# One output tile of the next quarter ahead of each loop over the rests of the counts, and a wait for attention's constants moved behind attention's first projection

## What is computed

```python
xn = layernorm(x)
# graph part: 20,000 edges, a self edge for every node
h   = xn @ W.T + b
out = segment_sum(deg**-0.5[row] * deg**-0.5[col] * h[col], row)
# attention part: 16 heads of 64, random features (exp of a projection)
q, k, v = xn @ Wq.T + bq, xn @ Wk.T + bk, xn @ Wv.T + bv
attn = phi(q) @ (phi(k).T @ v) / (phi(q) @ sum(phi(k)))
x = x + out + attn @ Wo.T + bo
# eight experts, the best two of each node are mixed
x = x + mixture_of_experts(layernorm(x))
```

## Time and profile before

| | |
|---|---|
| time, median of 3 runs | 1614.45 us (1612.59 to 1615.34) |
| the profiled execution, its own time | 1616.33 us |
| its span, first to last instruction | 1614.8 us |
| granted TensorE clock, mean | 0.949 |
| PE matmul busy | 1411.8 us, 87% of the span |
| DVE, ACT, POOL busy | 47%, 29%, 24% |
| graph stage, from the first matmul of line 1523 to the last | 312.9 to 449.7 us |
| share of PE in the chain that ended last | 76% |

### The profile page before, as it was taken

How to read it: one execution, slowest core, us unless ns; L and a number is a source line. 1 busy time by engine, 2 the same in 40 slices (tenths; PEclk the granted TensorE clock), 3 DMA queues, 4 the chain that set the end, 5 groups by cost and what they waited for, 6 DMA issues and landing times.

```text
span 1614.8 us, 26325 instructions
## 1 busy us (share of the span) xinstructions
PE 1411.8 (87%) x8396; PEld 1245.2 (77%) x8460; DVE 758.5 (47%) x1492; ACT 465.8 (29%) x777; POOL 383.8 (24%) x380
## 2 busy tenths in 40 slices
PE   5788878967879999999999999997999499999980
PEld 2566666967879999999999999996888488888860
DVE  7754443414334545444444545345454425444536
ACT  7412222401013333333232424243222113223310
POOL 7422343233221010101010101002224211222233
PEclk9999999988889999999999999999999599999995
DMA  4100111334222020202020202003144326665657
GB/s 150 54 32 23 53 59 56 97 115 123 84 71 85 20 90 14 91 13 91 13 91 13 91 13 78 0 1 120 57 144 139 141 74 237 239 238 215 213 199 279
DMA packets 64532, 158.06 MB, mean 98 GB/s; under 512 B 7978, under 2 KB 28922, under 8 KB 64032
## 3 DMA queue, kind: packets, MB, share of 16 engines
q1 hardware_dynamic: 55200, 127.20, 22.4%
q0 software_dynamic: 9280, 30.17, 6.0%
HBM read 119.98 MB, written 55.71 MB: 109 GB/s over the span
## 4 chain that ended last, share of the span: by engine, by line
PE 76%; DMA 7%; DVE 6%; issue 5%; ACT 2%; POOL 2%; DVEq 1%; SPq 1%; POOLq 0%; ACTq 0%
PE PB L1562 7%; PE PB L1564 7%; PE PB L1563 7%; PE PB L1738 5%; PE PB L1739 5%; PE PB L1741 5%; PE PB L1598 4%; PE PB L1621 4%; PE PB L1466 4%; DMA y_scratch<-xrow 3%; PE PB L1507 2%; PE PB L1544 2%; PE PB L1508 2%; PE PB L1509 2%; PE PB L1545 2%
## 5 line engine op out<-in xcount | busy, mean ns | idle before, releaser
L1562 PE MATMUL PB<-xh,hw 128*128 128x416 f32 (+1 forms) x576 | 206.0, 358 | 7.0 <-POOL orfl L758 7.0
L1564 PE MATMUL PB<-xh,hw 128*128 128x416 f32 (+1 forms) x576 | 204.1, 354 | 0.0
L1563 PE MATMUL PB<-xl,hw 128*128 128x416 f32 (+1 forms) x576 | 203.8, 354 | 0.0
L1738 PE MATMUL PB<-mwh,mth 128*128 128x512 f32 x368 | 149.4, 406 | 1.3 <-issue 1.3
L1466 PE MATMUL PB<-ohs,ohd 128*128 x471 | 107.4, 352 | 46.5 <-DVE ohs L1116 31.6
L1739 PE MATMUL PB<-mwl,mth 128*128 128x512 f32 x368 | 144.7, 393 | 0.0
L703 POOL CAST hw<-hraw 128x1024 fp32r<-128x1024 f32 x24 | 25.1, 1047 | 466.6 <-PE PB L1564 465.8
L1466 PEld LDWEIGHTS PB<-ohs,ohd 128*128 x534 | 52.3, 99 | 100.3 <-issue 82.3
L1562 PEld LDWEIGHTS PB<-xh,hw 128*128 128x128 f32 x576 | 109.4, 190 | 8.4 <-POOL orfl L758 7.2
L1741 PE MATMUL PB<-mwh,mtl 128*128 128x512 f32 x368 | 114.4, 392 | 0.0
L1563 PEld LDWEIGHTS PB<-xl,hw 128*128 128x128 f32 x576 | 109.5, 190 | 1.3
(11 more groups left out here) (260 smaller groups left out, 3135.3 us busy)
## 6 DMA issues: line engine op xcount, KB each, us to landing
mraw<-expert_w SPq DMA_DIRECT2D x64, 512.0 KB, 7.4
slot_y<-x SPq DMA_DIRECT2D x7, 2560.0 KB, 12.2
slot_y<-ybuf SPq DMA_DIRECT2D x46, 256.0 KB, 3.3
count_rests<-ATf POOLq DMA_DIRECT2D x9, 640.0 KB, 3.3
xrow<-x SPq DMA_DIRECT2D x40, 128.0 KB, 2.5
y_scratch<-xrow SPq DMA_DIRECT2D x40, 128.0 KB, 2.4
yrow<-y_scratch SPq DMA_DIRECT2D x20, 256.0 KB, 2.9
x2n_half<-xhat SPq DMA_DIRECT2D x20, 256.0 KB, 2.5
```

The costliest lines, as they stand in the source:

```text
L1562: mm(bank(i, n), hw[:, wi, 0, k, :], xh[:, k, c0:c0 + n], start=(k == 0), stop=False)
L1563: mm(bank(i, n), hw[:, wi, 0, k, :], xl[:, k, c0:c0 + n], start=False, stop=False)
L1564: ins = mm(bank(i, n), hw[:, wi, 1, k, :], xh[:, k, c0:c0 + n], start=False, stop=(k == KT - 1))
L1738: mm(y[c], mth[:, k, :], mwh[par][:, k, c * CW:(c + 1) * CW], start=(k == 0), stop=False)
```

## The change

On PE, DVE and POOL the loop over quarter q's rests now stands behind the first tile (t = 0) of quarter q + 1 and before its second; the last quarter's stays at the end. On POOL it was behind the second tile. PE's wait for `a_cst` stands behind `project(0, 0)`; ACT's and DVE's waits stay. The diff, without the lines that only move:

```diff
@@ POOL
             for u in range(TILES):
                 q = u // TT
+                if u % TT == 1 and u > TT:
+                    add_rests(q - 1)
                 pool.wait_ge(g_x[u % 4], 16 * (u // 4 + 1))
                 g.tensor_tensor(xrow[:, u % 4, :], xrow[:, u % 4, :], bob[:, q * QW:(q + 1) * QW], ALU.add).then_inc(xb_ready, 1)
                 if u in (TT, TT + 8):
                     split_head(0, (u - TT) // 8)
-                if u % TT == 1 and u > TT:
-                    add_rests(q - 1)
             add_rests(NQ - 1)
@@ DVE
             for u in range(TILES):
                 q, t = u // TT, u % TT
+                if t == 1 and q:
+                    take_rests(q - 1)
                 dve.wait_ge(g_done, u + 1)
                 dve.wait_ge(xb_ready, u + 1)
...
-                if t == TT - 1:
-                    with dve.Fori(0, rest_dve) as n:
...
+            take_rests(NQ - 1)
@@ PE
             for u in range(TILES):
                 q, t = u // TT, u % TT
+                if t == 1 and q:
+                    multiply_rests(q - 1)
...
                 ins.then_inc(g_done, 1)
-                if t == TT - 1:
-
-                    with pe.Fori(0, rest_pe) as n:
...
+            multiply_rests(NQ - 1)
@@ PE, attention
-
-            pe.wait_ge(a_cst, 7)
...
             project(0, 0)
+            pe.wait_ge(a_cst, 7)
             pairs(pe, pair)
```

More of the change, by code:

```diff
@@ L1152, in _, with take_rests @@
                     low_scaled(q, b)
+            def take_rests(q):
+                with dve.Fori(0, rest_dve) as n:
+                    b, at = rest_tile(n)
+                    k = rest_dve * q + n
+                    dve.wait_ge(rest_done, k + 1)
+                    dve.wait_ge(rest_over, k + START)
+                    v.tensor_scalar(resty[:, :], bank(3, QW), dis[:, ds(at, 1)], None, ALU.mult).then_inc(rest_taken, 1)
             for u in range(TILES):
                 q, t = u // TT, u % TT
+                if t == 1 and q:
+                    take_rests(q - 1)
                 dve.wait_ge(g_done, u + 1)
@@ L1512, in _, with multiply_rests @@
             rest_pe = rest_tiles(pe)
+            def multiply_rests(q):
+                with pe.Fori(0, rest_pe) as n:
+                    b, _ = rest_tile(n)
+                    k = rest_pe * q + n
+                    pe.wait_ge(rest_ready, 16 * (k + 1))
+                    pe.wait_ge(rest_taken, k + START)
+                    mm(bank(3, QW), restb[:, :], hh[:, q % 2, ds(b, 1), :].rearrange("p a n -> p (a n)"),
+                       start=True, stop=True).then_inc(rest_done, 1)
             for u in range(TILES):
                 q, t = u // TT, u % TT
+                if t == 1 and q:
+                    multiply_rests(q - 1)
                 at = slice(t * P, (t + 1) * P)
```

## The result

| | before | changed |
|---|---|---|
| time, median | 1613.52 us (4 runs) | **1597.35 us** (4 runs, 1596.04 to 1597.88) |
| ratio, 95% interval | | **0.9902** (0.9881 to 0.9922) |
| same comparison, beside e4, e5, e7 | 1614.24 us (11 runs) | 1603.15 us (6 runs), 0.9922 (0.9908 to 0.9936) |
| same comparison, beside e9, e10, e11 | 1615.85 us (9 runs) | 1599.73 us (5 runs), 0.9902 (0.9886 to 0.9918) |
| span of the profiled execution | 1614.8 us | 1596.3 us |

I had predicted 1602.6 us, with 1598.5 to 1609.0 as the range. The change is faster, as forecast, but by 16 us in the result's own comparison, and its time lies 1.2 us outside the range. Of the 5.3 us between forecast and time, 0.9 is the kernel before, whose median is 1613.52 us here and was 1614.45 when I predicted. Repeated, the change gave 11 and 16 us.

What follows compares the result with a forecast made beforehand. SP's ring was taken to pace the graph stage, with PE's wait for the constants ahead of attention. Borders -4.9 and constants -6.95 made -11.9 us; against 1614.45 that gave 1602.6 us, range 1598.5 to 1609.0.

Steps and rivals of the forecast that it cites:

- border 0/1: Between graph-stage quarters 0 and 1: rest loaded 0.6 us earlier, store of tile 11 0.1 us later; +1.7 with a slower DMA.
- border 1/2: Between graph-stage quarters 1 and 2: store of tile 21 1.3 us earlier, held by the load of hrf; ends -1.8 and +1.1.
- border 2/3: Between graph-stage quarters 2 and 3: rest loaded at 417.63 instead of 420.44, so the store of tile 31 3.7 us earlier.
- if that delay goes too, it is -5.1: Behind tile 31's store: the next load came 3.86 us later instead of 2.46; without that delay, -5.1 instead of -3.7 us.
- its cover: At attention's start: PE's first third, 7.72 us, would end 0.8 us behind the constants and so just hide them.
- the adding DMA: POOL's DMA in the chain of the rest at each border: issue to next addition put at 4.4, 6.04 and 3.44 us.
- Rival B: Adding DMA not held up by hrf, 3.44 us at each border: -0.9, -2.2 and -3.7, in all 1600.7 us; chance 0.12.
- SP's ring sets the pace: Graph stage: SP's stores and loads need 2.8 us a tile, PE 2.4, so most of PE's 34.9 us wait costs nothing.
- the constants' term: Attention's start: PE no longer waits for the constants ahead of its first projection, which starts 6.95 us earlier.
- rival D: Borders: a lost tile of lead lets the ring run dry, 6.4 us each; slower, 1626.7 us; chance 0.04.
- My far bounds: The fast ends of two terms: -6.8 us for the three borders, -7.2 us for the wait for the constants.
- rival C: Attention's start: DVE meets POOL's 2.37 us instruction, PE waits and 2.4 us go back, 1605.0 us; chance 0.06.

Runs made afterwards that it cites:

- e4: The changed kernel with the two loads of hrf issued from ACT's queue instead of SP's; 1604.99 us, ratio 0.9940 to the kernel before.
- e5: The changed kernel with POOL no longer waiting for the adding DMA's landing; ACT waits and signals instead; 1601.34 us, ratio 0.9919 to the kernel before.
- e7: The changed kernel with the diffs of e4 and e5 together; 1600.79 us, ratio 0.9908 to the kernel before.
- e9: The changed kernel with the last rest's matmul behind the first third of attention's first projection on PE; 1599.10 us, ratio 0.9905 to the kernel before.
- e10: The changed kernel with the diffs of e9 and e5 together; 1594.50 us, ratio 0.9868 to the kernel before.
- e11: The changed kernel with 16 matmuls without use on PE in its wait ahead of the last rest; 1599.20 us, ratio 0.9897 to the kernel before.
- e1: The kernel before with only PE's wait for the constants moved, the loops over rests left in place; 1608.74 us, ratio 0.9952.
- e3: The changed kernel with POOL's loop over rests again behind its addition of t = 1; 1602.29 us, ratio 0.9917 to the kernel before.
- e6: e2 with 50 matmuls without use on PE ahead of the wait for the constants; 1608.27 us, ratio 0.9952 to the kernel before.
- e2: The changed kernel with PE's wait for the constants put back, so only the loops moved; 1608.28 us, ratio 0.9956 to the kernel before.
- e8: The changed kernel again, unchanged, run beside e4, e5 and e7; ratio 0.9922 to the kernel before.
- e12: The changed kernel once more, unchanged, run beside e9, e10 and e11; ratio 0.9902 to the kernel before.

## Why the prediction was wrong, and what of it was right

The table sets my terms beside the profiles. The old order of the graph stage has two (the kernel before, and the one with only the constants moved, e1), the change has three. A border is from the store of tile 10 q - 1 to that of 10 q + 1; "quarters" are the rest of the first three.

| stretch, us | old order | change | difference of means | my term |
|---|---|---|---|---|
| border 0/1 | 10.95, 11.75 | 12.64, 12.25, 12.11 | +1.0 | +0.1 |
| border 1/2 | 11.77, 12.85 | 12.04, 12.16, 12.15 | -0.2 | -1.3 |
| border 2/3 | 11.00, 11.50 | 8.00, 8.09, 8.11 | -3.2 | -3.7 |
| store of tile 31 to last addition | 17.80, 17.89 | 15.49, 15.53, 15.66 | -2.3 | 0 |
| last addition to projection | 10.85 | 3.58, 3.66, 3.71 | -7.2 | -6.95 |
| first projection | 16.79 | 14.31, 15.86, 15.69 | -1.5 | 0 |
| quarters | 73.6, 74.5 | 71.0, 74.8, 72.3 | -1.4 | 0 |
| sum | | | -14.8 | -11.9 |

The steps of the prediction that failed are two gains that I put at nothing, 2.3 and 1.5 us, and one cost that I took too short, 2.5 us the other way.

- **The slow landing behind tile 31, the largest.** I wrote "if that delay goes too, it is -5.1" and put it at the end of the range. It went in all three profiles of the change (1.72 us in the one shown, against 3.86) and was there in both of the old order (3.53 in the second), so it belonged in the sum: -2.3 us. It is no mere scatter either: it is tied to the order of the steps. In all eight profiles with POOL's loop ahead of tile 31 and its wait for the landing, the store landed in 1.7 us; in the other six (before, e1, e3, e5, e7, e10) it took 2.9 to 4.1. What goes with it is a 16 KB packet of the kind "instruction". It stands among the DMAs between the store's issue and its landing in the kernel before (431.19 to 435.05; packets, MB, share):

```profile
q1 hardware_dynamic: 288, 0.26, 22.7%
q8 instruction: 1, 0.02, 1.5%
```

It does not in the change (426.33 to 428.05):

```profile
q1 hardware_dynamic: 144, 0.13, 22.9%
```

In the six the packet begins 0.4 to 2.0 us behind the store's issue, and the store lands 2.1 to 2.6 us behind the packet's start; in the eight it begins 0.6 to 2.0 us ahead of the issue. Over all 14 profiles, leaving out stores beside hrf or beside the weights at tile 15, 23 of 106 stores that met such a packet took over 2.75 us, and none of the 408 that met none. No run moved the packet alone, so that it is the cause is likely and not shown.
- **The clock, a step that I did not take at all.** I counted the projection's first third at 7.72 us in the changed kernel, as the earlier trace rows has it behind 6.95 us of idle time, and its cover (ACT 0.8 us behind the constants) with it. With the wait gone the idle time ahead of the last rest is 2.0 to 2.7 us, and PE is either not slowed (14.31 us in the change's first profile, 14.1 to 14.3 in e3, e4, e5 and e7) or slowed for 10 matmuls (15.86 and 15.69; in e1 for 8, 15.67). e6 shows that the slow matmuls are the clock: kept busy, PE does not have them. Against the kernel before that is 0.9 to 2.5 us by profile, 1.5 in the mean. But the kernel before has one profile, and e2, with the same wait, took 15.81, as long as two of the three of the change. So the moved wait's share of the clock is nothing to 2.5 us, by profile.
- **Borders 0/1 and 1/2: the adding DMA was taken too short.** I took 4.42 and 6.04 us from before; it took 5.2 to 5.9 and 7.5 to 7.7. At border 1/2 it now goes 0.4 us behind the issue of hrf and went 2.7 behind it before. At border 0/1 that distance hardly changed (2.6 and 2.9), and why it took longer there is open; in e1, in the old order, it took 4.73 and 6.92, so some of this is scatter. I also let it go at the moment at which the store had landed, and POOL needed 0.8 us more (420.72 to 421.52). These cost 2.5 us against my sum. Rival B, an adding DMA that hrf does not hold up, is refuted: 3.5 us alone, 7.6 beside it.
- The two omissions were gains and the third point a loss; with the quarters, where the change's own three differ by 3.8 us, the sum came out 2.9 us too small. Of the quarters' -1.4 us, 0.8 lie in quarter 0, ahead of everything that moved, and can't be the change's. What is left of the first comparison's 16.2 us I take for scatter: its profile has no landing of a store over 2.75 us apart from those behind a larger load, e8's has two, of 4.71 and 3.41 us.
- **Right:** that SP's ring sets the pace and most of PE's wait is its slack; the constants' term, 7.0 against 7.2; that they are hidden behind PE; the place of the gain at border 2/3, though e3 takes my reason for it away; that a tile's lead on POOL is lost with little effect (rival D: +1.0 at the first border, the one that I had called "at the point").
- The range was too narrow on its fast side. My far bounds, -6.8 and -7.2, made -14.0; I added a microsecond or two for the run and had no room for a term that I had not seen. The ratio 0.9902 of the 1614.45 that I reckoned from is 1598.6, on the range's edge: how far outside the result fell is in part the run's luck.

## What to carry to other kernels

Where a wait of PE is shortened, the work behind it is to be priced at the clock that it will then have: look at the granted clock from the wait's start to where it is full again, and count the slow matmuls there as part of the wait, as a range, since one kernel gave 14.3 and 15.9 us for the same projection. A landing that is late in one row and prompt in the others is to be looked into before it is called chance: what else was under way, and will the change move it? A DMA that many steps wait for is to be priced beside the large transfer that it will meet in its new place, not beside the one that it met before. And once an experiment shows that a hold moves with its cause, as the one by the load of hrf did when another queue issued it, no sum should be built on removing it.

## What the runs showed of the hardware

**The clock's fall is not decided by the idle time alone.** PE's gap ahead of the last rest was 2.48, 2.60, 2.61 and 2.68 us in the kernel before, e8, e1 and e12, and the clock fell; it was 1.86, 2.02, 2.32 and 2.41 us in e3, the change, e4 and e7, but also 2.51 and 2.54 us in e5 and e6, and it stayed. In e8 and e12 it fell late: PE had been at work again for 1.5 and 1.2 us (448.15 to 449.66, 446.32 to 447.52). Nor does the same wait cost the same: at work again behind 6.95 us of idle time, PE did 16 slow matmuls in the kernel before (granted clock 0.50 still from 464 to 465 us, 1.00 from 466), and 10 behind 6.83 us in e2.

**A DVE instruction with one input is stretched beside POOL.** I had brought this up as rival C for DVE's instructions with two inputs. In the changed kernel POOL and DVE meet:

```profile
453.44 2.41 POOL L705 TENSOR_TENSOR hw<-hraw,hw 128x1024 fp32r<-128x1024 f32 x1
```
```profile
453.22 0.37 DVE L1210 CAST tk<-qf 64x418 fp32r<-64x418 f32 x1 [7.01 <-ACT qf L955]
453.60 2.48 DVE L1211 CAST tk<-qf 64x418 fp32r<-64x418 f32 x1
```

Two casts of the same size, 0.37 and 2.48 us; the second ends 0.2 us behind POOL's instruction. PE did not wait for it, as it had a whole projection to do first, so rival C did not come about.

**A small transfer is not spared a large one in another queue.** A 128 KB store from SP's queue took 7.2 us beside 1,280 KB from ACT's queue (e4), 2.4 alone.

**A late landing of a small store goes with an instruction packet.** 23 of 106 stores of 128 KB that had a packet of the kind "instruction" beside them took over 2.75 us; of 408 without one, none did (stores beside hrf or the weights left out).
